# Feed-forward of a fused attention and expert kernel: down products two chunks back and first in the chunk, and TensorE's four matmul signals per chunk replaced by one drain with a signal

## What is computed

```
q, k, v = x@Wq+bq, x@Wk+bk, x@Wv+bv                 # 16 heads of 8
for each window of 64 tokens, stride 32 (and the last 64 tokens once more):
    probs = softmax(q_w k_w^T / sqrt(8) + pos_bias);  merged[window] += probs v_w
x = layernorm(x + (merged / counts) @ Wo + bo)

logits = x @ router_w.T;  the best 2 of 8 experts, g = sigmoid(logit), normalised over the two
out = sum over experts e of g_e * ((silu(x @ w_gate[e]) * (x @ w_up[e])) @ w_down[e])
x = layernorm(x + out)
```

## Time and profile before

| what | value |
|---|---|
| median of 3 runs | 729.98 us (729.13 to 731.42) |
| profiled execution | span 841.8 us; no other time of it is given |
| PE busy | 671.6 us (80%), 13466 instructions |
| DVE busy | 504.7 us (60%) |
| POOL busy | 437.6 us (52%) |
| ACT busy | 365.0 us (43%) |
| granted clock, mean | 0.902 |

### The profile page before, as it was taken

How to read it: one execution, slowest core, us unless ns; L and a number is a source line. 1 busy time by engine, 2 the same in 40 slices (tenths; PEclk the granted TensorE clock), 3 DMA queues, 4 the chain that set the end, 5 groups by cost and what they waited for, 6 DMA issues and landing times.

```text
span 841.8 us, 33526 instructions
## 1 busy us (share of the span) xinstructions
PE 671.6 (80%) x13466; PEld 525.3 (62%) x13466; DVE 504.7 (60%) x1622; ACT 365.0 (43%) x544; POOL 437.6 (52%) x486
## 2 busy tenths in 40 slices
PE   4589999999999989999999978866778787887300
PEld 1356666666667666666666657866677777886300
DVE  6647766777676757786677653655444444544274
ACT  2134434444444434444443334634344445554165
POOL 6522155546545526555654563555555555455465
PEclk9699999999999969999999986989979999989655
DMA  6884454464345434456454030322233222221294
GB/s 167 240 243 117 125 154 123 131 174 133 119 137 137 151 100 131 120 138 188 123 132 125 27 79 30 116 63 72 70 105 90 77 76 78 73 70 58 71 408 152
DMA packets 83576, 103.54 MB, mean 123 GB/s; under 512 B 15488, under 2 KB 70144, under 8 KB 83424
## 3 DMA queue, kind: packets, MB, share of 16 engines
q1 hardware_dynamic: 67008, 70.20, 29.7%
q0 software_dynamic: 8640, 17.84, 6.6%
q10 hardware_dynamic: 7776, 13.37, 4.4%
HBM read 60.12 MB, written 40.79 MB: 120 GB/s over the span
## 4 chain that ended last, share of the span: by engine, by line
PE 54%; issue 14%; DVE 13%; another core or an unknown queue 7%; ACT 4%; POOL 3%; DMA 2%; ACTq 1%; SPq 0%; DVEq 0%; POOLq 0%
PE o_ps L1374 6%; PE score_ps L1316 4%; PE ctx_ps L1388 4%; PE scoret_ps L1334 4%; PE score_ps L1327 4%; PE o_ps L1368 3%; PE bank L1243 3%; PE o_ps L1498 3%; PE bank L1301 3%; DVE neg_max L853 3%; PE scoret_ps L1351 3%; PE scoret_ps L1316 2%; PE ctx_ps L1498 2%; DVE h_sb L1116 2%
## 5 line engine op out<-in xcount | busy, mean ns | idle before, releaser
L304 POOL DMA_INDIRECT slots<-rows_sb,slot_at x128 | 129.8, 1014 | 153.1 <-PE o_ps L1374 96.0
L569 POOL DMA_INDIRECT results<-scaled_sb,result_at x142 | 136.5, 961 | 122.8 <-DVE scaled_sb L1127 86.8
L853 DVE TENSOR_REDUCE neg_max<-score_ps 128x16 f32<-128x1024 f32 x109 | 132.8, 1218 | 90.6 <-PE score_ps L1316 88.5
L729 ACT ACTIVATE prob<-scoret_ps 128x1024 f32<-128x1024 f32 x109 | 111.7, 1025 | 147.8 <-PE scoret_ps L1316 134.4
L1374 PE MATMUL o_ps<-v_sb,prob 128*64 128x18 f32 x2048 | 77.9, 216 | 3.7 <-issue 3.6
L1374 PEld LDWEIGHTS o_ps<-v_sb,prob 128*64 128x64 f32 x2048 | 73.8, 147 | 4.8 <-issue 4.4
L765 ACT CAST w_slot<-wgu_sb 128x1024 fp32r x71 | 74.9, 1056 | 0.3 <-issue 0.3
L1388 PE MATMUL ctx_ps<-diag,o_sb 128*64 128x64 f32 x896 | 57.4, 242 | 16.3 <-DVE o_sb L868 11.6
L1334 PE MATMUL scoret_ps<-bias_hl,fold 128*128 128x512 f16 x218 | 68.6, 398 | 0.0
L1388 PEld LDWEIGHTS ctx_ps<-diag,o_sb 128*64 128x64 f32 x896 | 40.6, 142 | 36.1 <-issue 29.0
L1498 PE MATMUL o_ps<-wd_sb,h_sb 128*128 x288 | 43.5, 299 | 20.7 <-DVE h_sb L1116 18.1
(11 more groups left out here) (188 smaller groups left out, 1599.5 us busy)
## 6 DMA issues: line engine op xcount, KB each, us to landing
stack<-scratch SPq DMA_DIRECT2D x32, 512.0 KB
blocks<-scratch SPq DMA_DIRECT2D x126, 128.0 KB
scratch<-qk_hl SPq DMA_DIRECT2D x92, 128.0 KB
xin<-slots SPq DMA_DIRECT2D x71, 130.0 KB
blocks<-results ACTq DMA_DIRECT2D x16, 512.0 KB, 9.7
scratch<-qk_hl ACTq DMA_DIRECT2D x36, 128.0 KB
x_sb<-in_x SPq DMA_DIRECT2D x16, 256.0 KB
out<-y_sb SPq DMA_DIRECT2D x16, 256.0 KB, 3.4
```

Of the source, the lines that this page charges most:

```text
L304: nc.gpsimd.indirect_dma_start(slots, bass.IndirectOffsetOnAxis(ap=slot_at[:, k % 2, n:n + 1], axis=0), rows_sb[:, k % 2, n // TT, n % TT, ...
L569: pool.indirect_dma_start(results, bass.IndirectOffsetOnAxis(ap=result_at[s % RBUF][:, t:t + 1], axis=0), scaled_sb[:, s % RBUF, t, :], No ...
L729: act.activation(prob[:, (par + u) % 2, :], turned_scores(i, u)[:, :, :].rearrange("p b c -> p (b c)"), ACT.Exp).then_inc(exp_done, 1)
L853: dve.tensor_reduce(neg_max[:, par, :, v, :], ps[:, :, :].rearrange("p b (h k) -> p b h k", k=W), AX_X, ALU.max, negate=True).then_inc(max ...
```

## The change

- PE's order in iteration s becomes down(s-2), gate_up(s), turn(s+2), then a drain of PE that raises the single semaphore chunk_ps. The two down products that are left behind the loop have a drain with a signal each. The table read of chunk s stands at the iteration's head, so behind the drain of chunk s-1.
- gate_ps, up_ps and y_ps are gone, and xt2_ps is signalled for the first two chunks alone. silu(s), hidden(s) and high(s+2) wait for chunk_ps at s+1; weights_in for the count of three chunks back, as before; scale(s) for s+3, the drain behind down(s). Waits which chunk_ps or the order already imply are left out of high, low and hidden.
- PE's products for the last attention step (project_out and others) stand behind the drain of their chunk. POOL runs deviation of the last step ahead of the first stores.

```diff
@@ POOL, behind the attention steps
                 for s in range(SLOT_CHUNKS):
-                    results_out(s)
                     if s == 0:
                         deviation(STEPS - 1)
+                    results_out(s)
@@ ACT
                 def weights_in(s, e):
-                    after(act, up_ps, s + 1 - WBUF)
+                    after(act, chunk_ps, s + 1 - WBUF)
...
                 def high(s):
-                    act.wait_ge(xt2_ps, s + 1)
-                    after(act, up_ps, s + 1 - HBUF)
+                    if s < 2:
+                        act.wait_ge(xt2_ps, s + 1)
+                    else:
+                        act.wait_ge(chunk_ps, s - 1)
...
                 def silu(s):
-                    act.wait_ge(gate_ps, s + 1)
+                    act.wait_ge(chunk_ps, s + 1)
                     after(act, h_done, s - 1)
@@ DVE
                 def low(s):
                     dve.wait_ge(x_high, s + 1)
-                    after(dve, up_ps, s + 1 - HBUF)
...
                 def hidden(s):
                     dve.wait_ge(silu_done, s + 1)
-                    dve.wait_ge(up_ps, s + 1)
-
-                    after(dve, y_ps, s + 1 - HBUF)
+                    dve.wait_ge(chunk_ps, s + 1)
...
                 def scale(s):
-                    dve.wait_ge(y_ps, s + 1)
+                    dve.wait_ge(chunk_ps, s + 3)
@@ PE
-                    last.then_inc(xt2_ps, 1)
+                    if s < 2:
+                        last.then_inc(xt2_ps, 1)
+                    return last
...
-                    for n, signal in ((0, gate_ps), (1, up_ps)):
+                    for n in range(2):
...
-                        last.then_inc(signal, 1)
+                    return last
...
-                    last.then_inc(y_ps, 1)
+                    return last
...
                 for s in range(SLOT_CHUNKS):
                     if s == FIRST:
                         pe.wait_ge(tables, 2)
-                    e_before, e_of = e_of, table_value(pe, expert_at, s, E - 1)
-                    gate_up(s)
+                    e_of.append(table_value(pe, expert_at, s, E - 1))
+
+                    if s >= LATE:
+                        down(s - LATE, e_of[s - LATE])
+                    last = gate_up(s)
+                    if s + 2 < SLOT_CHUNKS:
+                        last = turn(s + 2)
+                    pe.drain().then_inc(chunk_ps, 1)
                     if s == 0:
                         project_out(STEPS - 1)
...
-                    if s + 2 < SLOT_CHUNKS:
-                        turn(s + 2)
-                    if s:
-                        down(s - 1, e_before)
-                down(SLOT_CHUNKS - 1, e_of)
+                for s in range(SLOT_CHUNKS - LATE, SLOT_CHUNKS):
+                    down(s, e_of[s])
+                    pe.drain().then_inc(chunk_ps, 1)
```

More of the change, by code:

```diff
@@ L243, in build @@
         fill_made, tables_begun = sem("fill_made"), sem("tables_begun")
-        gate_ps, up_ps, silu_done, h_done = sem("gate_ps"), sem("up_ps"), sem("silu_done"), sem("h_done")
-        y_ps, scaled, result_out = sem("y_ps"), sem("scaled"), [sem(f"result_out{n}") for n in range(RBUF)]
+        chunk_ps, silu_done, h_done = sem("chunk_ps"), sem("silu_done"), sem("h_done")
+        scaled, result_out = sem("scaled"), [sem(f"result_out{n}") for n in range(RBUF)]
         final_in = [sem(f"final_in{n}") for n in range(AHEAD)]
@@ L1518, in _ @@
                 pe.wait_ge(tables, 1)
-                e_of = None
+                e_of = []
                 for s in range(SLOT_CHUNKS):
```

## The result

The change takes 808.33 us (median of 5 runs, 807.82 to 813.2), the kernel before beside it 731.42 us (5 runs, 729.13 to 735.25). The ratio is 1.106, with a 95% interval of 1.102 to 1.110: 77 us slower. Each time here is a median of all runs, and each ratio is of the runs within 1.5% of their kernel's fastest. The forecast was 798 us, its range 750 to 862.

What follows compares the result with a forecast made beforehand. POOL's stores were taken to bound the feed-forward at 206 us; after the change PE would, at 262.7 + 2.5 + 8.6 = 273.8 us. The 68 us difference on 729.98 gave 798 us, range 750 to 862.

Steps and rivals of the forecast that it cites:

- The floor: Feed-forward without stalls: POOL's indirect DMAs and small operations end the last store 206 us after the stretch's start.
- The gap: PE behind each drain: 0.03 us for the drain, 0.95 for table read and following steps to the first down matmul.
- The size of a chunk: PE's feed-forward chunk goes from 2.55 to 3.70 us, 1.15 more; bounds 0.76 to 1.4 more.
- the two other terms, 2.5 and 8.6: Beside PE's chunks: 2.5 us for the last attention step's products, 8.6 for stores behind the last full chunk.
- Down products two chunks back and first: PE's order in the feed-forward: removes its wait for h_sb, 35 us in the trace; taken as zero gain.
- Fewer signals: Three fewer matmul signals a chunk: nothing by the rows, 5.6 us back by a skill-page estimate.
- Later starts: silu waits for the whole chunk, 0.7 + 0.2 us more; x_lo still ready before PE needs it, hidden by 1.3 us.
- The stalls, and whose they are: Late PE signals in attention and feed-forward, 119 us of the profile's span, are nearly absent from the timed runs.
- 841.8 - 119: Profile span less lateness, 46 us in attention and 73 in feed-forward: 723 us, within 1% of the 729.98 median.
- the profiled stretch hardly longer than its 271.4 us: Sign: the changed feed-forward's profile may hardly exceed 271.4 us, since stalls only the profile has lie there already.
- The held drain: Rival: late signals hold each feed-forward drain up to 0.9 us in timed runs, 64 us more, 862 us; chance 0.09.
- The clock: Rival: PE's clock falls from 2.4 to 1.2 GHz, chunk 6.25 us, kernel about 980 us; chance 0.04.

Runs made afterwards that it cites:

- e12: The change with its single signal on the chunk's last matmul (last transpose) instead of the drain, on chip D: 734.61 us, 1.004 of the kernel before.
- e9: The kernel before with every indirect DMA of attention issued twice, the copy into a buffer nothing reads, on chip D: 793.29 us, ratio 1.081.
- e11: The change with the next chunk's table read moved ahead of the drain, which stays, on chip D: 761.38 us, 1.037 of the kernel before.
- e4: The kernel before with a bare drain of PE, without signal, at the end of each iteration, on chip B: 852.93 us, ratio 1.018.
- e8: The kernel before with down products written two chunks back and first, four matmul signals kept, no drain, on chip C: 840.98 us, ratio 1.001.
- e10: The change with both the early table read and the signal on the last transpose instead of a drain, on chip D: 734.39 us, ratio 1.003.
- e2: The change with its single signal on the chunk's last matmul instead of the drain, on chip B: 828.74 us, 0.989 of the kernel before.
- e6: The change with its single signal on the chunk's last matmul instead of the drain, on chip C: 823.5 us, 0.988 of the kernel before.
- e1: The kernel before, unedited, profiled once more on chip B: 842.76 us for the profiled execution, span 840.0 us.
- e3: The change with the next chunk's table read moved ahead of the drain, which stays, on chip B: 818.72 us, 0.977 of the kernel before.
- e5: The change, unedited, run once more on chip C: 857.98 us, 1.022 of the kernel before.

## Why the prediction was right, and which step was not

*The floor.* It was taken as 206 us and e12 shows 207. The whole kernel before was profiled only where its signals are late, so e12, equal to it in time within 0.8%, stands in for it. The feed-forward of e9, which is before's on a chip with prompt signals, agrees: its chunks are 2.55 us apart at the median.

*The gap.* The pause was forecast as 0.03 + 0.95 = 0.98 us and is 0.97 (0.99 at the median); e11 shows that 0.63 of it is the table read, e4 that the drain brings it by itself. The missing cover was the right mechanism.

*The size of a chunk.* Forecast 3.70, measured 3.82. The term that was too small is the first matmul behind the gap: the eight records of the down products take 1.15 us in the change and 1.06 in e12, 0.09 us that the sum had only in its upper bound. 71 x 0.12 = 8.5 us. From the first gate product to the end of the last store the forecast was 273.8 us; it is 279.5, since the two other terms, 2.5 and 8.6, came to 8.3 together and so were 3 us too large. That is 72 us over e12's, where 68 were forecast. Where the other 5 of the 77 lie is not shown: the change's feed-forward begins at 484.8 us and e12's at 478.6, but the change's profiled execution (813.2 us) is itself 5 us above its median, and e12 lies 2.7 us above before.

*Down products two chunks back and first: zero.* The number is right and its working is not. The prediction has this part take away PE's wait for h_sb, worth up to 35 us; e8 shows that the part moves no product and that the wait stays (33.8 us). The "35 us at the other end" never existed, and that zero was chosen is luck as far as the order goes.

*Fewer signals: zero.* Right where signals are prompt: e12 and e10 lie within 1% of before and not below it. PE's chunk is 2.55 us at the median with four signals (e9) and with one (e12). The 5.6 us, an estimate from the Trainium skill, TensorE: Matmul & The Clock Gate, "The cost: per-tile semaphore tail", would be 0.08 us of it and did not show. Where signals are late, the single signal is worth 1.1 to 1.2% (e2, e6).

*Later starts.* Hidden, as forecast: in the change's trace PE does not wait for x_lo in the feed-forward, and for h_sb only twice, 1.8 us in all.

**The step that failed** is the one under "The stalls, and whose they are": that the timed runs hold nearly none of the stalls, because they belong to the profiled execution. For the chip that gave the result its number holds. Its reason does not: e1's span of 840.0 us has a time of 842.8 beside it, after's 811.1 has 813.2. The profile of before must have shown a condition in which the kernel takes about 836 us, while the three runs beside it came from one in which it takes 731; this is concluded from the match with e1, for the record names neither chip. Had the change been timed on B or C, the forecast of 68 us more would have been wrong; on C it is 22. That 841.8 - 119 came within 1% of the median was also helped by chance: the 13 attention steps were counted as 46 us of lateness, but where signals are prompt such a step still takes 28.0 us (364.0 / 13) and not 26.1, and the feed-forward begins 37.5 us earlier in e12 than in the trace of before. The forecast "the profiled stretch hardly longer than its 271.4 us" came true for another reason too: the change was profiled where signals are prompt (273.6), before where they are late.

*The held drain,* the rival at 862 us. On the result's chip drains are held for 1.7 us in all. On C the kernel takes 858 us, near the rival's figure and not by its working: 11.7 us of held drains, not 64; most of the rest is time ahead of the feed-forward, which begins at 512.4 us there, where it begins at 484.8 in the result's trace and at 516.1 in e8.

*The clock* did not fall: 0.99 over the feed-forward.

What stays open: what differs between the chips (or the moments at which they were used), whether the signal or the matmul behind it is late, and whether POOL's indirect DMAs cause the lateness or only meet it.

## What to carry to other kernels

A drain on TensorE ended 0.02 us behind the last matmul where signals are prompt; what it costs is the sequencer's work that used to run ahead of the matmuls and now stands behind it. Of the 1.27 us a chunk it cost here, 0.68 went with the table read, so whatever can be read before the drain belongs before it; 0.59 stayed with the drain, and a signal on the last matmul is better still where signals are prompt. Before a gap between a profile's span and the timed runs is put down to the recording, the same kernel should be profiled again with its time beside it, because the profile may come from another chip. A stall that one chip shows can hide most of a loss (22 us of 77 were left), so the verdict on a change should name the chip's time of the kernel before. And before a reordering is given a price, the list of the engine should be written out across the edge of the loop: a product moved from the end of one iteration to the head of the next has not moved.

## What the hardware did that was not expected

Signals given by matmuls land late on some chips. On B and C more than half of the feed-forward's signals land late, with the kernel before and with e8 (148 of 263, 157 of 265), the one looked at above by 6.3 us; on D none of 286 is, in e9, whose feed-forward is that of before. In attention the shares are 131 of 581 on B and 29 of 596 on D (e12). The same kernel takes 836 us on two of the chips and 731 to 732 on D and beside the result.

The late ones keep to POOL's indirect DMAs. In e1, between 108 and 500 us, of the matmuls with a signal that end while such a DMA runs 88 of 129 have it over 0.15 us late, of those that end within 1.5 us behind one 63 of 212, and elsewhere none of 130; in e12 the same counts are 28 of 173, 11 of 211 and 1 of 114. None of the recorded signals of ACT and DVE is late. This is a correlation, and e9 could not make more of it. Such a DMA is not enough by itself: in the feed-forward of e9 220 of the matmuls with a signal end while one runs, and none is over 0.3 us late; in that of e4, on the slow chip but with a drain a chunk, 20 of 138 are, and in e1's 109 of 155.

The signal of a drain was not found late: it lands 0.01 us behind the drain's end on B too (e3), and it is the drain that is held (26.1 us in all there, 11.7 in e5). This fits the change being 10.6% slower in the result and but 2.2% slower on C: there the kernel before pays for late signals all through the feed-forward, and the change hardly does.
